# Strip transfers of two attention operands issued in two halves of four blocks each

## What is computed

```python
xn = ada_ln(x, t_emb, ln1_g, ln1_b, aff1_w, aff1_b)
x = x + mha(xn, xn, xn, sa_qw, sa_qb, sa_kw, sa_kb, sa_vw, sa_vb, sa_ow, sa_ob)   # 512 keys
x = x + mha(x, u, u, ca_qw, ca_qb, ca_kw, ca_kb, ca_vw, ca_vb, ca_ow, ca_ob)      # 77 keys
xn = ada_ln(x, t_emb, ln2_g, ln2_b, aff2_w, aff2_b)
x = x + (gelu(xn @ ffn_w1 + ffn_b1) @ ffn_w2 + ffn_b2)
```

## Time and profile before

| | us |
|---|---|
| timed runs, median of 3 | 283.95 |
| lowest, highest | 279.34, 284.93 |
| the profiled execution | 277.5 |
| its span from first to last instruction | 275.7 |
| TensorE busy | 230.2 (84% of the span) |
| ScalarE busy | 157.9 (57%) |
| VectorE busy | 153.1 (56%) |
| GpSimd busy | 54.8 (20%) |

### The profile page before, as it was taken

How to read it: one execution, slowest core, us unless ns; L and a number is a source line. 1 busy time by engine, 2 the same in 40 slices (tenths; PEclk the granted TensorE clock), 3 DMA queues, 4 the chain that set the end, 5 groups by cost and what they waited for, 6 DMA issues and landing times.

```text
span 275.7 us, 3963 instructions
## 1 busy us (share of the span) xinstructions
PE 230.2 (84%) x1299; PEld 98.8 (36%) x1302; DVE 153.1 (56%) x374; ACT 157.9 (57%) x280; POOL 54.8 (20%) x136
## 2 busy tenths in 40 slices
PE   2978799995898989896898876599779999978982
PEld 1323243431133222221322243232226555553752
DVE  7589587877468867893611457500323461362633
ACT  4353387766368767874898631448622784333730
POOL 5389951023001017211310012200100100100000
PEclk9999999999579999997999999959856999999998
DMA  7964160313010000330000000000000000001001
GB/s 277 394 239 114 52 217 16 102 23 96 0 36 0 4 0 4 115 98 23 2 8 2 0 2 2 2 5 1 0 0 1 2 1 0 0 2 38 0 0 38
DMA packets 6616, 13.20 MB, mean 48 GB/s; under 512 B 1926, under 2 KB 4806, under 8 KB 6182
## 3 DMA queue, kind: packets, MB, share of 16 engines
q1 hardware_dynamic: 5014, 9.03, 9.6%
q0 software_dynamic: 1584, 3.94, 4.6%
HBM read 8.07 MB, written 4.69 MB: 46 GB/s over the span
## 4 chain that ended last, share of the span: by engine, by line
PE 57%; DVE 14%; DMA 10%; ACT 6%; POOL 6%; issue 5%; SPq 2%; DVEq 0%; ACTq 0%; POOLq 0%
PE UP L782 7%; DVE negm L1246 5%; PE ST L756 4%; DMA KS<-scr_k 4%; PE S L730 4%; PE ST L986 3%; PE UP L785 3%; PE ST L981 3%; PE S L937 3%; ACT PT L1068 3%; DMA QX<-scr_q 3%; DMA QS<-mT 2%; PE ST L1005 2%; PE ST L759 2%; PE S L942 2%
## 5 line engine op out<-in xcount | busy, mean ns | idle before, releaser
L1068 ACT ACTIVATE PT<-ST 128x512 f32<-128x512 f32 (+1 forms) x160 | 86.5, 596 | 32.7 <-PE ST L756 24.8
L1246 DVE TENSOR_REDUCE negm<-S 128x1 f32<-128x512 f32 x128 | 79.7, 683 | 25.1 <-PE S L730 25.1
L730 PE MATMUL S<-KS,QS 48*128 48x512 bf16 x128 | 38.5, 392 | 8.9 <-DVE negm L1246 4.6
L756 PE MATMUL ST<-QS,KS 51*128 51x512 bf16 x128 | 39.7, 394 | 1.0 <-DMA QS<-mT 0.7
L782 PE MATMUL UP<-PT,VS 128*32 128x512 f32 x256 | 36.7, 647 | 0.0
L756 PEld LDWEIGHTS ST<-QS,KS 51*128 51x128 bf16 x128 | 10.3, 94 | 35.5 <-issue 30.8
L577 POOL CAST mpart<-negm 128x16 bf16<-128x16 f32 x16 | 3.2, 199 | 95.9 <-DVE negm L1246 55.8
L1250 DVE TENSOR_REDUCE negm<-S 128x4 f32<-128x308 f32 x32 | 13.2, 471 | 9.7 <-PE S L736 9.7
L730 PEld LDWEIGHTS S<-KS,QS 48*128 48x128 bf16 x128 | 9.6, 94 | 24.1 <-issue 17.5
L645 POOL TENSOR_TENSOR rstd<-rstd,half 128x4 f32<-128x4 f32 x4 | 4.1, 1018 | 61.1 <-DVE rstd L1297 61.1
L736 PE MATMUL S<-KX,QX 48*128 48x77 bf16 x128 | 6.8, 197 | 6.8 <-DVE negm L1250 3.4
(11 more groups left out here) (278 smaller groups left out, 353.8 us busy)
## 6 DMA issues: line engine op xcount, KB each, us to landing
w_late<-late SPq DMA_DIRECT2D x1, 3089.5 KB, 11.7
scr_q<-part POOLq DMA_DIRECT2D x2, 384.0 KB, 3.6
QS<-scr_q SPq DMA_DIRECT2D x2, 384.0 KB
KS<-scr_k SPq DMA_DIRECT2D x2, 384.0 KB
QX<-scr_q POOLq DMA_DIRECT2D x2, 384.0 KB, 6.5
xn<-x_nat SPq DMA_DIRECT2D x2, 256.0 KB, 3.7
xT<-x_T SPq DMA_DIRECT2D x1, 512.0 KB, 12.6
scr_q<-part POOLq DMA_DIRECT2D x2, 256.0 KB, 3.4
```

Source lines behind the costliest of these rows:

```text
L730: last = mm(S[:, n % 3, :], QS[r, b, 2 * g + jj, i * P:(i + 1) * P], KS[r, b, 2 * g + jj, :], start=True, stop=True)
L756: mm(ST[:, k % 3, :], KS[r, b, block, kt * P:(kt + 1) * P], QS[r, b, block, :], start=True, stop=True).then_inc(s["st_ready"], 1)
L1068: a(PT[0:rows, n % 2, j, :], ST[0:rows, k % 3, :], ACT.Exp, scale=SCALE).then_inc(s["exp_out"], 1)
L1246: v.tensor_reduce(negm[:, slot, e // 4, e % 2, e // 2 % 2:e // 2 % 2 + 1], S[:, n % 3, :], AX.X, ALU.max, negate=True).then_inc(s["max_out ...
```

## The change

Three strip sets are divided by blocks: the first four blocks (groups 0 and 1) and the last four (groups 2 and 3). strips() gets an end k1, and a row of a half is 4 KB.

- For element 1 the steps strips_q1 (round 3) and strips_k1 (round 7) become strips1 with half 0 (round 3) and half 1 (round 7). Each issues the Q and the K strips of its half: four transfers of 192 KB instead of two of 384 KB. The two waits of the K strips now stand in both.
- For element 0's cross queries GpSimd issues the two halves one after the other in the same step.
- Each half has its own semaphore, and the maxima of groups 0 and 1 wait for half 0 alone, those of groups 2 and 3 for half 1.

```diff
@@ -155,8 +155,8 @@
-    put(3, 0, ("strips_q1",))
-    put(7, 0, ("strips_k1",))
+    put(3, 0, ("strips1", 0))
+    put(7, 0, ("strips1", 1))
@@ -472,12 +472,12 @@
-        def strips(eng, dst, scr, done, k0=0):
+        def strips(eng, dst, scr, done, k0=0, k1=H // 2):
 
             for q in range(2):
                 src = scr[:, 64 * q:64 * q + 64, :].rearrange("i (d k) t -> i d k t", d=DH)
-                eng.dma_start(dst[STRIP * q:STRIP * q + STACK, k0:, :].rearrange("p k t -> p (k t)"),
-                              src[:, :, k0:, :].rearrange("i d k t -> i d (k t)")).then_inc(done, 16)
+                eng.dma_start(dst[STRIP * q:STRIP * q + STACK, k0:k1, :].rearrange("p k t -> p (k t)"),
+                              src[:, :, k0:k1, :].rearrange("i d k t -> i d (k t)")).then_inc(done, 16)
@@ -504,13 +504,13 @@
-                elif step[0] == "strips_q1":
+                elif step[0] == "strips1":
+                    k = step[1] * GROUPS
                     sp.wait_ge(s["stack_q1"], STACK_DMAS)
-                    strips(sp, QS[:, 1, :, :], scr_q[1], s["strips_1"])
-                elif step[0] == "strips_k1":
+                    strips(sp, QS[:, 1, :, :], scr_q[1], s[f"strips_1_{step[1]}"], k, k + GROUPS)
                     sp.wait_ge(s["late_set"], 1)
                     sp.wait_ge(s["stack_k1"], STACK_DMAS)
-                    strips(sp, KS[:, 1, :, :], scr_k[1], s["strips_1"])
+                    strips(sp, KS[:, 1, :, :], scr_k[1], s[f"strips_1_{step[1]}"], k, k + GROUPS)
@@ -614,7 +614,8 @@
                     pool.wait_ge(s["stack_qx0"], STACK_DMAS)
-                    strips(g, QX[:, 0, :, :], scr_q[B], s["strips_qx0"])
+                    for k in (0, GROUPS):
+                        strips(g, QX[:, 0, :, :], scr_q[B], s[f"strips_qx0_{k // GROUPS}"], k, k + GROUPS)
@@ -714,9 +715,9 @@
                 elif kind == SELF:
-                    pe.wait_ge(s["strips_1"], 2 * STRIP_DMAS)
+                    pe.wait_ge(s[f"strips_1_{g // 2}"], 2 * STRIP_DMAS)
                 elif b == 0:
-                    pe.wait_ge(s["strips_qx0"], STRIP_DMAS)
+                    pe.wait_ge(s[f"strips_qx0_{g // 2}"], STRIP_DMAS)
                     pe.wait_ge(s["strips_kx"], STRIP_DMAS)
```

More of the change, by code:

```diff
@@ L445, in block_program @@
             block_ready block_act block_dve qf_ready qf_out split1
-            stack_q0 stack_k0 strips_0 stack_q1 stack_k1 stack_qx0 stack_kx strips_1 strips_qx0 xblock_ready xblock_act
+            stack_q0 stack_k0 strips_0 stack_q1 stack_k1 stack_qx0 stack_kx strips_1_0 strips_1_1 strips_qx0_0 strips_qx0_1 xblock_ready xblock_act
             ctx_ready ctx_v_ready kxf_out split_x strips_kx vx_out kT1_out v1_out
```

## The result

The changed kernel takes 268.7 us as the median of four executions (267.57 to 275.64), the kernel before 283.2 (four, 279.34 to 284.93). The ratio is 0.955, with a 95% interval of 0.941 to 0.969. The prediction was 274.4 us, with a range of 268 to 280 and 0.72 on faster. So the direction was right and the measured median lies inside the range, 0.7 us from its fast end: 14.5 us were gained where 9.5 were forecast. A repetition (after_again, six executions against seventeen) gave 271.2 against 281.8, 10.6 us, with a ratio of 0.958. So a part of the 14.5 may be the chance of four executions on each side.

The account below looks back on a forecast made before the run. TensorE was taken to be held up by its waits for KS and QX, each idle time plus slow clock. 6.3 + 3.2 = 9.5 us off the 283.95 us median gave 274.4 us, range 268 to 280.

Parts of the forecast that it names:

- Reading of the bound: TensorE's waits for KS and QX, each idle time plus a slow-clock stretch, both lie on the path.
- First wait: TensorE waiting for KS at element 1's first maxima: 3.3 us idle plus about 3.0 of slow clock, 6.3 us.
- the x8 round: Round with the larger part of the weight folding (L874 x8), near the KS wait, put at 3.36 us undisturbed.
- Second wait: TensorE waiting for QX at element 0's first cross maxima: 2.2 us idle plus slow clock, priced at 3.2 us.
- the round taken as plain: Third of the rounds around the QX wait, assumed to take 2.72 us undisturbed.
- I take the same 9.5 off the median: Carries the saving summed from the profile to the timed runs: median 283.95 us becomes 274.4.
- Strips on SyncE: Element 1's halves arrive early: first with 8 to 10 us of cover, second with 17; maxima rows keep 0.7 and 0.8.
- The 89 of the earlier trace: GB/s of SyncE's pair of whole strip transfers over 60 to 69 us, used to time the halves.
- "clogged" rival: Halved rows on SyncE's queue take 18 us a set instead of 9 and delay maxima rows: 288.4 us; chance 0.05.
- The halves of QX: Element 0's first cross-query half lands at 123.7 to 124.2 against a need at 124.3, so its wait goes.
- The estimate from the Trainium skill's page: About 2.0 us fixed per transfer; if costs add up, the first pair leads by only 0.9 us, sum 7.2 us.
- The slow clock comes anyway: Rival: TensorE's slow stretches only move, so only idle time, 5.5 us, is gained: 278.4 us; chance 0.15.

Follow-up runs that it names:

- after_again: The changed kernel, unedited, timed again; 271.2 us median over six executions, ratio 0.958 to the kernel before.
- self_only: The changed kernel with QX in two whole transfers again, only element 1's strips divided; 273.9 us against 283.3 before, ratio 0.964.
- qx_only: The kernel before with QX alone in two halves, each with its own semaphore; 275.4 us, ratio 0.985 to the kernel before.
- the filler: The kernel before with 14 products nobody reads ahead of element 1's first maxima, during the KS wait; 279.5 us against 281.8, ratio 0.990.
- k_early_whole: The kernel before with element 1's whole K strips moved from round 7 to round 3, nothing divided; 281.8 us against 283.3.
- after: The changed kernel as first measured; 268.7 us median of four executions, its profiled execution 269.1 us.
- after_fill: The changed kernel with 8 and 6 unread products in two TensorE waits for VectorE's normalisation; 266.7 us, ratio 0.939 to the kernel before.
- after_fill2: The changed kernel with 14 unread products in two normalisation waits and six more in the wait for the first maxima split; 266.4 us, ratio 0.945.
- qx_joint: The changed kernel, but the first cross maxima wait for both halves of QX; 272.0 us, ratio 0.969 to the kernel before.

## Why the prediction was right, and which term was mis-sized

**Reading of the bound.** Right. Both waits were on the path, and taking away either gave its own share (self_only, qx_only).

**First wait.** 6.3 us forecast, 6.5 by the same three rounds, since the x8 round takes 3.16 us undisturbed and not 3.36. The split into 3.3 idle and 3.0 slow clock held: the filler gained 3.3.

**Second wait.** 3.2 forecast and 3.1 in the profiles compared (the round taken as plain, 2.72, takes 2.90). This is the term that was mis-sized for the timed runs. The prediction took the slow stretch behind QX from one execution, 3.7 us at 0.54. A second profile has 20 us, and a price of 9.1 us in place of 3.1; the mean price of six profiles is 5.1. The profiled execution of before, 277.5 us, was one of the fastest of that kernel (two of 55 were faster), so its price was a low one. The prediction saw that its median lay 6.5 us higher and took the same 9.5 us off both; the step "I take the same 9.5 off the median" is the one that failed. The 6.5 us should have been asked for their place: they were partly in the very term that the change removes. Over all executions the kernels differ by 12.6 us in the mean, 3.0 more than by terms. The 2.0 that the price of QX lies higher in the mean of six profiles are the larger part of that; the rest, slow stretches elsewhere, is not traced term by term.

**The number.** 268.7 lies in a range that ends at 268, and that is partly luck: the repetition's 271.2 lies 3.2 us under the forecast and the first 5.7, and nothing in the working had a price for that spread.

**Strips on SyncE.** Their cover was underrated in one point: half sets move faster than I took. The second set was at work from about 61 to 67 us, not 60 to 69:

```profile
62.00:67.00 5.00, 4.64 (x36) 1.32 (x33) 4.76 (x10) 4.07 (x9) 2.35 (x12) 1.00 0.37 147
```

147 GB/s, where the same five microseconds of before had 116, at the same small share of the engines (0.37 and 0.38). The 89 of the earlier trace rows is over nine microseconds, both ends of the transfer included; over 60 to 69 us the changed kernel has 90, for the same bytes. The tail of the second half therefore never reached the maxima rows of group 3. The "clogged" rival named a real place (k_early_whole shows the rows of group 2 held up by strips), but its condition was wrong: halved rows took less time, not more.

**The halves of QX.** Forecast to land at 123.7 to 124.2 against a need at 124.3. Landings of the four transfers, by issue in the trace of after (KB each, median us):

```profile
QX<-scr_q POOLq DMA_DIRECT2D x4, 192.0 KB, 4.2
```

Their extremes were 3.3 and 4.9 us, as in the earlier trace rows, and the first cross maxima start at 118.66 without a wait for them, as in the four other profiles with this edit (qx_only, after_again, after_fill, after_fill2). The estimate from the Trainium skill's page "DMA: Bandwidth & Descriptors", fixed costs that add up so that the first pair is only 0.9 us ahead, did not come true: the wait that vanished was 2.2 us, and with the short rows even the whole set was 1.1 us nearer (qx_joint).

**The slow clock comes anyway.** It did in a small way: the dip at slice 8, 1.0 us. The waits' stretches did not simply move. But the dip may belong to the change. Five of the seven profiles that ask for element 1's K strips in round 3 have one at this place of the program (after, k_early_whole, qx_joint, after_fill, after_fill2), with rounds 1.0 to 2.5 us longer in all, and none of the six that ask for them in round 7 has one. No run was made to test this.

## What to carry to other kernels

Cost a stall of TensorE as idle time plus the slow stretch behind it, and take that stretch from more than one execution: here it was 4 or 20 us behind the same wait. Where the timed median lies well above the profiled execution, look for the difference in the terms that the change touches before carrying a sum from one to the other. Where an idle time can't be removed, products that nobody reads, written to a bank that is free or about to be overwritten, kept the clock up in most places and brought the medians down by 2 to 8 us here.

## What was not expected of the hardware

- On SyncE's queue 4 KB rows in four transfers went faster than 8 KB rows in two: 9.3 us from first issue to last landing in one profile against 10.4 to 11.1 in five, for 768 KB. Whether it is the row or the number of transfers under way that does it was not tried.
- A wait of 0.67 us was followed by a slow stretch in k_early_whole, one of 1.07 us in qx_joint was not. In the changed kernel the clock fell near 52 us, with TensorE busy throughout, right behind fourteen products of two columns (L861, 49.69 to 51.41); in the first profile of before the same products were followed by no fall. What decides stays open, beyond the count given above by the round in which the K strips are asked for.
